# Moving the fourth expert bank from VectorE to ScalarE and GpSimd in steps 32 to 34

## The reference

```python
x = x + 0.5 * ffn(layernorm(x))    # 8 experts, D=256 -> 256, top 2 of 8 by softmax gates
x = x + attn(layernorm(x))         # 16 heads of 16, each row attends to itself and two neighbours
x = x + 0.5 * ffn(layernorm(x))    # the same expert weights
```

## Time and profile before

| what | value |
|---|---|
| device time, median of 3 runs | 1085.56 us (1085.13 to 1087.37) |
| profiled execution | 1084.92 us, span 1083.1 us |
| mean granted TensorE clock | 0.991 of 2.4 GHz |
| busy: PE, DVE, ACT, POOL | 95%, 80%, 50%, 66% |

### The profile page before, as it was taken

One profiled execution on the slowest core, in us unless ns is written; L12 is line 12 of the kernel. 1 busy time (PEld: TensorE's weight loads), 2 busy tenths in 40 slices (PEclk: granted clock), 3 DMA queues, 4 the chain that ended last, 5 costly groups with the idle time before them and its releaser, 6 DMA issues.

```text
span 1083.1 us, 17734 instructions
## 1 busy us (share of the span) xinstructions
PE 1032.8 (95%) x5277; PEld 849.9 (78%) x5277; DVE 862.6 (80%) x2405; ACT 544.1 (50%) x1219; POOL 714.4 (66%) x956
## 2 busy tenths in 40 slices
PE   5889899999999999999999999999999999999885
PEld 3677788888888888888888888888888888887663
DVE  3648888888888888887888888788988888888882
ACT  4264455554455555454555554455555554544331
POOL 3366577776668776766777766677766667664353
PEclk9899999999999999999999999999999999999998
DMA  5001000000000000000000000000000000000000
GB/s 170 11 28 38 15 20 20 2 20 21 20 20 21 20 15 7 21 21 21 20 20 21 6 16 21 20 20 21 20 16 6 20 21 20 11 10 11 11 11 20
DMA packets 12616, 23.04 MB, mean 21 GB/s; under 512 B 2245, under 2 KB 5845, under 8 KB 12521
## 3 DMA queue, kind: packets, MB, share of 16 engines
q1 hardware_dynamic: 9240, 13.37, 3.5%
q0 software_dynamic: 3280, 8.53, 2.8%
HBM read 12.46 MB, written 8.39 MB: 19 GB/s over the span
## 4 chain that ended last, share of the span: by engine, by line
PE 88%; DVE 6%; issue 2%; DMA 1%; ACT 1%; SPq 0%; POOL 0%; POOLq 0%; ACTq 0%; DVEq 0%
PE ffn_bank L910 20%; PE ffn_bank L912 20%; PE ffn_bank L911 20%; PE tr_bank L939 5%; PE mix_bank L910 4%; PE mix_bank L912 4%; PE mix_bank L911 4%; PE tr_bank L952 3%; PE mix_bank L984 2%; PE tr_bank L910 1%; DMA we_raw<-in_L_ffn_We 1%; PE tr_bank L911 1%; PE tr_bank L912 1%; PE tr_bank L959 1%; DVE chain_sum L678 1%
## 5 line engine op out<-in xcount | busy, mean ns | idle before, releaser
L910 PE MATMUL ffn_bank<-we_hi,T_hi 128*128 128x512 f32 x1024 | 410.2, 401 | 3.7 <-DVE chain_sum L678 3.0
L912 PE MATMUL ffn_bank<-we_hi,T_lo 128*128 128x512 f32 x1024 | 401.6, 392 | 0.0
L911 PE MATMUL ffn_bank<-we_lo,T_hi 128*128 128x512 f32 x1024 | 401.0, 392 | 0.0
L470 ACT ACTIVATE we_raw<-ffn_bank,gate 128x256 f32<-128x256 f32 x512 | 206.9, 473 | 163.2 <-PE ffn_bank L912 116.9
L346 POOL TENSOR_TENSOR chain_sum<-chain_sum,we_raw 128x512 f32<-128x512 f32 x128 | 166.1, 1298 | 126.3 <-DVE chain_sum L678 123.7
L910 PEld LDWEIGHTS ffn_bank<-we_hi,T_hi 128*128 128x128 f32 x1024 | 193.3, 189 | 43.5 <-DVE chain_sum L678 3.9
L912 PEld LDWEIGHTS ffn_bank<-we_hi,T_lo 128*128 128x128 f32 x1024 | 192.9, 188 | 42.0
L911 PEld LDWEIGHTS ffn_bank<-we_lo,T_hi 128*128 128x128 f32 x1024 | 193.4, 189 | 35.3
L678 DVE SCALAR_TENSOR_TENSOR chain_sum<-ffn_bank,gate,we_raw 128x256 f32<-128x256 f32 x256 | 111.7, 477 | 62.2 <-ACT we_raw L470 35.4
L678 DVE SCALAR_TENSOR_TENSOR chain_sum<-ffn_bank,gate,chain_sum 128x256 f32<-128x256 f32 x256 | 111.4, 477 | 37.7 <-PE ffn_bank L912 37.7
L323 POOL TENSOR_TENSOR var_eps<-mean_var,eps 128x2 f32<-128x2 f32 x96 | 28.8, 300 | 151.0 <-DVE mean_var L599 151.0
(11 more groups left out here) (128 smaller groups left out, 1655.5 us busy)
## 6 DMA issues: line engine op xcount, KB each, us to landing
out_x<-y SPq DMA_DIRECT2D x31, 256.0 KB
we_raw<-in_L_ffn_We SPq DMA_DIRECT2D x2, 1024.0 KB, 14.2
x_in<-in_L_attn_x,x_row POOLq DMA_INDIRECT x60
x_in<-in_L_attn_x SPq DMA_DIRECT2D x2, 256.0 KB, 8.2
moved_qk<-qk SPq DMA_DIRECT2D x4, 124.0 KB
w_raw<-in_L_attn_Wq SPq DMA_DIRECT2D x1, 256.0 KB, 2.9
w_raw<-in_L_attn_Wk SPq DMA_DIRECT2D x1, 256.0 KB, 3.1
w_raw<-in_L_attn_Wv SPq DMA_DIRECT2D x1, 256.0 KB, 4.7
```

Of the source, the lines that this page charges most:

```text
L470: last = nc.scalar.activation(scaled[:, f, t, half, j], ffn_bank[b][:, j * D:(j + 1) * D], ACT.Copy, scale=gate[:, 2 * f + t, e:e + 1])
L910: nc.tensor.matmul(dest, hi[:, t, k, :], w_hi_[:, k, c0:c1], start=(first and k == 0), stop=False, skip_group_check=not first)
L911: nc.tensor.matmul(dest, hi[:, t, k, :], w_lo_[:, k, c0:c1], start=False, stop=False, skip_group_check=not first)
L912: last = nc.tensor.matmul(dest, lo[:, t, k, :], w_hi_[:, k, c0:c1], start=False, stop=(k == KB - 1), skip_group_check=not first)
```

## The change

For groups 28, 29 and 30 (steps 32, 33 and 34) VectorE no longer handles bank 3. ScalarE scales it instead (`fourth_step`, right behind `scale_step` of the same tile) into the buffer that FFN1 used for its scaled bank 2, which is free by then. GpSimd adds it in `sum_step` with one more 128x512 addition behind L346. VectorE's second operation for bank 1 counts `chain_done` up by 3, so all who wait for the full chain are released at that point. TensorE waits for ScalarE's `fourth_done` instead of the chain before it overwrites bank 3. ScalarE waits for GpSimd's `fourth_added` before it writes the buffer again.

```diff
+        def act_fourth(f, n):
+            return f == FFN2 and PAIRS <= n.const + 4 < LAST_STEP
+        def fourths(n, t):
+            return 2 * (n.const + 4 - PAIRS) + t + 1
...
                 pool.wait_ge(done, n.times(2 * RESIDUAL_SUMS, RESIDUAL_SUMS * t + 1))
+                if act_fourth(f, n):
+                    pool.wait_ge(fourth_done, fourths(n, t))
+                    nc.gpsimd.tensor_tensor(chain_sum[:, f, t], chain_sum[:, f, t], scaled[:, FFN1, t, 1], ALU.add).then_inc(fourth_added, 1)
+                    pool.wait_ge(fourth_added, fourths(n, t))
                 pool.wait_ge(base_done[f], n.times(1, 1))
...
+            def fourth_step(n, t):
+                if n.const + 4 == PAIRS:
+                    act.wait_ge(sum_done[FFN1], PAIRS * 2 * RESIDUAL_SUMS)
+                else:
+                    act.wait_ge(fourth_added, fourths(n - 1, t))
+                act.wait_ge(bank_full[FFN2], n.times(8, 4 * t + 4))
+                for j in range(2):
+                    last = nc.scalar.activation(scaled[:, FFN1, t, 1, j], ffn_bank[3][:, j * D:(j + 1) * D],
+                                                ACT.Copy, scale=gate[:, 2 * FFN2 + t, 6 + j:7 + j])
+                last.then_inc(fourth_done, 1)
...
                     scale_step(FFN2, s - 4, 0)
+                    if act_fourth(FFN2, s - 4):
+                        fourth_step(s - 4, 0)
...
                     scale_step(FFN2, s - 4, 1)
+                    if act_fourth(FFN2, s - 4):
+                        fourth_step(s - 4, 1)
...
-                                                   op0=ALU.mult, op1=ALU.add).then_inc(done, 1)
+                                                   op0=ALU.mult, op1=ALU.add).then_inc(
+                                                       done, 3 if j == 1 and act_fourth(f, n) else 1)
...
-                if ffn2:
+                if ffn2 and not act_fourth(FFN2, s - 4):
                     chain_step(FFN2, s - 4, 0, 3)
...
-                if ffn2:
+                if ffn2 and not act_fourth(FFN2, s - 4):
                     chain_step(FFN2, s - 4, 1, 3)
...
-                    if b % 2:
+                    if b == 3 and act_fourth(g, m):
+                        pe.wait_ge(fourth_done, fourths(m, u))
+                    elif b % 2:
                         await_(pe, chain_done[g], m.times(8, 4 * u + b + 1))
```

More of the change, by code:

```diff
@@ L207, in build @@
         bank_full = [sem(f"bank_full{f}") for f in range(NF)]
+        fourth_done, fourth_added = sem("fourth_done"), sem("fourth_added")
         scaled_done = [sem(f"scaled_done{f}") for f in range(NF)]
```

## The result

The changed kernel took 1089.59 us (median of 10 runs, 1087.98 to 1090.51), the kernel before 1086.06 us (10 runs, 1085.13 to 1088.24). The ratio is 1.0029, with a 95% interval of 1.0019 to 1.0039, so by the ratio the change costs 3.1 us (2.1 to 4.2); the two medians are 3.5 us apart. That is slower, by about 0.3%, though the lower end of the interval lies just under the 0.2% named above. The forecast of 1087.7 us was 2.1 us above the median known then, a ratio of 1.0019. The range, 1083.6 to 1090.0 us, held, with the measured median near its upper end.

The account below looks back on a forecast made before the run. The prediction took VectorE to lead in steps 32 and 33, TensorE to follow. Collisions of 0.57 + 0.27 + 0.05 = 0.9 us and 1.2 us for one clock drop gave +2.1 us, 1087.7 us; range 1083.6 to 1090.0 us.

Parts of the forecast that it names:

- What bounds the kernel there: Steps 32 and 33: VectorE leads, TensorE follows; step 34: VectorE has 4.5 us idle, worth nothing; ScalarE's added work costs nothing.
- The gain ahead of the products: Step 32, VectorE: L723 ends near 1014.05 instead of 1015.28, so exp, scaling and the next pair start 1.23 us earlier.
- L731's wait: Step 32, tile 1: L731 on VectorE waits for GpSimd's L355, making the products 0.1 us later.
- The turns: GpSimd's four tile 1 operations alternate with VectorE's products and sums; in step 32 `attn` ends 2.1 us later.
- The rival in which the back-to-back products keep GpSimd out: L742 operations let no GpSimd operation between them, so L355 falls behind `attn`: -0.3 us, 1085.3 us, chance 0.15.
- The low part: Behind step 32's `attn`, L604 (`lo_step(TO)`) starts at 1024.88 instead of 1024.31, 0.57 us late.
- Step 33: `attn` ends at 1044.85 instead of 1042.50, L604 comes 0.84 us late in all, 0.27 us of it added here.
- the 0.05 us of step 35: The longer GpSimd sums of step 34 reach the gate part of step 35 0.05 us later.
- The gaps: TensorE stands idle ahead of `attn` for 3.6 us in step 32 and 3.35 us in step 33.
- The clock: TensorE's granted clock drops to 0.50 behind a gap, 1.2 us each; one drop of two possible counted as likeliest.
- its second case: Collisions between GpSimd and VectorE plus one drop or two of TensorE's clock: +2.1 or +3.3 us, 1087.7 to 1088.9 us, chance 0.38.
- The other side: GpSimd does not hold up VectorE's products: 2.8 us gained in each of steps 32 and 33, -5.6 us, 1080.0 us, chance 0.12.

Follow-up runs that it names:

- the kernel with the late group: The changed kernel, but in steps 32 and 33 GpSimd's four operations for tile 1 wait until VectorE has written `attn`; 1084.30 us, ratio 0.9978.
- Tile 0 alone: The changed kernel, but only tile 0's bank 3 moves and tile 1's stays on VectorE; 1083.20 us, ratio 0.9976 against the kernel before.
- the kernel with the filled gap: The changed kernel, but in steps 33 and 34 TensorE computes bank 1 of tile 0 three times; 1086.51 us, ratio 1.0007 against the kernel before.
- the kernel with both tiles and the later group: The changed kernel, but in steps 32 and 33 GpSimd's tile 1 operations wait for all gate parts of the next step; 1088.54 us, ratio 1.0017.
- the narrow add: The changed kernel, but in steps 32 and 33 GpSimd's new add for tile 1 covers 2 of 256 columns of each half; 1085.76 us, ratio 0.9997.
- tile 1 alone: The changed kernel, but only tile 1's bank 3 moves and tile 0's stays on VectorE; 1093.82 us, ratio 1.0069 against the kernel before.

## Why the prediction was right, and where it was off

- **What bounds the kernel there** held. Step 34 was worth nothing that can be told (0.9998), and ScalarE's work cost nothing that was seen: the kernel with the late group carries all of it and is 2.4 us faster than before.
- **The gain ahead of the products** was forecast at 1.23 us, less 0.1 us for L731's wait. The products' start, less the shift, is 1017.05, as the forecast had it: 1.13 us gained. Tile 0 alone shows this gain by itself, without the loss.
- **The turns.** `attn` 2.1 us late in step 32, measured 2.00. The rival in which the back-to-back products keep GpSimd out is refuted: three of them took 4.50 us with GpSimd between. The low part 0.57 us late: 0.91 us, of which the slow transposes have 0.46 (1.12 against 0.66 us), so 0.45 us. Step 33 adds 0.16 us (1.83 less 1.67) where 0.27 us were forecast. Together 0.6 instead of 0.84 us (0.9 us with the 0.05 us of step 35); the kernel with the filled gap gives 0.8 us for this part by its ratio and 0.72 us by its trace.
- **The gaps** were forecast at 3.6 and 3.35 us and measured at 3.50 and 3.25 us.
- **The clock.** A drop was priced at 1.2 us. Measured: in step 33 1.22 us (x2 1.67 late, less 0.45), in step 34 1.27 us (3.10 less 1.83). The term that was off is their number. The forecast counted one; the profiled execution has two. Over all ten executions of the changed kernel the mean granted clock is 0.9856, over the sixty of the kernel before that were timed with the experiments 0.989, and with the filled gap it is back at 0.9885. Half clock for 3.4 us takes 0.0016 off such a mean, so the difference of 0.0033 fits two drops on average, by this estimate; whether every execution has both is not shown. With two the forecast's sum is 0.9 + 2.4 = 3.3 us, which the prediction names as the other half of its second case; measured were 2.94 us in the profile and 3.1 us by the ratio. So the small miss is two misses that partly cancel: the turns were put 0.2 to 0.3 us too high and the number of drops one too low. The forecast stood at the edge of what a measurement can tell, and the second drop carried it over, so the chances leaned a little too far to no change.
- **The other side**, a gain of 5.6 us, would have needed GpSimd to leave VectorE alone. It does not: its group met the products in the changed kernel, the gate part when it started behind `attn`, and the scores when it started later still, and none of the kernels tried gained more than 2.6 us.

## What to carry to other kernels

A step moved off the bound engine also moves what waited for it: here three old operations on GpSimd started 5.4 us earlier (1016.85 instead of 1022.27), right into VectorE's operations on two SBUF tensors. They stretched the products more than the added operation did (1.53 against 1.07 us) and account for about 2.1 of the 5.5 us that a later start of the group gives back; the added one, with the drops that it brings, accounts for the rest. When an engine becomes free early, look at what it will run beside, not only at how long it works; move the part whose followers run beside PSUM reads (tile 0: 2.6 us gained, faster than both kernels) and leave the other. And a longer wait ahead of TensorE can cost more than its own length: behind each traced wait of 3.25 us and more in steps 33 and 34 the clock dropped, for another 1.2 to 2.4 us. Between 2.2 and 2.5 us the traces show both, no drop behind 2.2 and 2.5 us in one kernel and a drop behind 2.5 us in another, so no safe length can be read from them.

## What the runs showed of the hardware

- GpSimd gets its turn even between VectorE operations that follow each other without a wait: three 128x512 products took 4.50 us instead of 1.90, and 3.43 us with only a 128x4 add as the second of the four GpSimd operations.
- TensorE's granted clock fell to 0.50 behind waits of 3.50, 3.25, 3.37, 4.17 and 4.24 us, and behind one of 2.51 us in the kernel with both tiles and the later group. It did not behind 2.5 and 2.2 us in steps 33 and 34 of the profiled execution with the narrow add. So the length of the wait alone does not tell.
- It stayed low for 3.4 us behind the waits of 3.50, 3.25 and 2.51 us and for 6.8 us behind those of 3.37, 4.17 and 4.24 us. A drop of 3.4 us cost 1.22 and 1.27 us in the changed kernel, one of 6.8 us 2.4 and 2.0 us with tile 1 alone. The low stretch began up to 1.2 us behind the end of the wait (step 34 of the changed kernel) or up to 1.8 us ahead of it (step 34 with tile 1 alone).
